# First stage of a decoder kernel: scores over 64 rows in pairs of banks, outputs in one bank, and a power on GpSimd for root and reciprocal

## The reference

```python
r, k, v, g = xr @ w_r.T, xk @ w_k.T, xv @ w_v.T, silu(xg @ w_g.T)   # xr.. are x mixed with x one token back
# per head, in chunks of tokens:
y = rr @ kk * Wmat @ vv + rr @ state * wb        # scores, masked by decay, times values; plus the carried state
state = ws * state + kk * wk @ vv
mu, var = y.mean(-1), y.var(-1)                  # over the 16 channels of a head
y = (y - mu) / jnp.sqrt(var + EPS)
y = y * ln_g + ln_b
y = y * g
x = _layernorm(x + y @ w_o.T)
```

## Time and profile before

| | us |
|---|---|
| three runs | 2878.19, 2883.38, 2891.40; median 2883.38 |
| the profiled execution, own time | 2882.24 |
| its span, from the first to the last instruction | 2880.9 |
| first stage, from the span's start | 0 to 279.5 |
| TensorE, VectorE, ScalarE, GpSimd busy in the first stage | 227.8, 183.9, 53.3, 69.3 |
| TensorE, VectorE, ScalarE, GpSimd busy in the whole span | 2227.3, 1720.4, 1181.4, 598.3 |

### The profile page before, as it was taken

The page is one execution under the profiler, slowest core; times in us unless marked ns, Lnnn a source line. Parts: engine busy times, 40 slices in busy tenths (PEclk is TensorE's granted clock), DMA queues, the critical chain, the costliest instruction groups (busy, mean ns, idle before and its releaser), DMA issues. The chain is left out here.

```text
span 2880.9 us, 41338 instructions
## 1 busy us (share of the span) xinstructions
PE 2227.3 (77%) x15516; PEld 1433.2 (50%) x15582; DVE 1720.4 (60%) x3425; ACT 1181.4 (41%) x2185; POOL 598.3 (21%) x488
## 2 busy tenths in 40 slices
PE   6995469897506999365589999996787787778777
PEld 3553137674404888334235555554455544455534
DVE  5676975467783333357456666661677652677663
ACT  2121664334331333121223555554566442566443
POOL 2220000001173455501310000000322142322052
PEclk9997579999657999687779999997899898899999
DMA  3001400100161111212431111102000001000000
GB/s 108 1 1 31 136 1 1 44 1 1 45 228 45 45 46 45 70 29 44 132 106 36 35 33 27 35 13 88 1 1 1 11 1 58 1 1 1 17 31 23
DMA packets 75010, 113.28 MB, mean 39 GB/s; under 512 B 22853, under 2 KB 59681, under 8 KB 74145
## 3 DMA queue, kind: packets, MB, share of 16 engines
q1 hardware_dynamic: 71744, 102.24, 11.8%
q0 software_dynamic: 3072, 8.39, 0.9%
HBM read 85.38 MB, written 31.20 MB: 40 GB/s over the span
## 5 line engine op out<-in xcount | busy, mean ns | idle before, releaser
L2338 DVE TENSOR_REDUCE xa_max<-psum 128x1 f32<-128x1024 f32 (+1 forms) x256 | 248.5, 988 | 130.0 <-PE psum L2211 129.3
L2444 ACT ACTIVATE xa_work<-psum 128x1024 f32<-128x1024 f32 (+1 forms) x208 | 212.7, 1023 | 188.6 <-PE psum L2234 186.7
L2249 PE MATMUL psum<-xa_work,xa_values 128*33 128x128 f32 (+1 forms) x3328 | 224.0, 277 | 0.0
L2249 PEld LDWEIGHTS psum<-xa_work,xa_values 128*33 128x33 f32 (+1 forms) x3328 | 168.1, 111 | 73.7 <-issue 70.2
L2644 PE MATMUL psum<-wqkv_l,x_hl_l 128*128 128x512 bf16 x538 | 136.9, 400 | 65.7 <-POOL x_hl_l L2904 32.9
L3010 PE MATMUL psum<-h_ch_f,w_f 128*128 128x512 bf16 (+1 forms) x556 | 134.9, 396 | 34.3 <-issue 13.1
L1623 DVE TENSOR_SCALAR moe_raw<-psum,tile_b 128x256 f32<-128x256 f32 x184 | 78.3, 475 | 138.9 <-PE psum L1465 137.9
L1719 POOL TENSOR_TENSOR x_ch<-moe_raw,x_ch 128x512 bf16<-128x512 f32 x92 | 105.4, 1156 | 151.9 <-ACT x_ch L1679 149.9
L1465 PE MATMUL psum<-moe_rows,moe_w 128*128 128x256 bf16 x1104 | 132.5, 278 | 3.0 <-POOL moe_rows L1715 3.0
L2234 PE MATMUL psum<-xa_query_rows,xa_key_rows 98*128 98x512 bf16 (+1 forms) x416 | 127.2, 388 | 8.4 <-ACT xa_work L2444 7.7
L2211 PE MATMUL psum<-xa_key_rows,xa_query_rows 96*128 96x512 bf16 (+1 forms) x512 | 127.0, 344 | 4.5 <-DVE xa_max L2338 2.4
(11 more groups left out here) (415 smaller groups left out, 4934.7 us busy)
## 6 DMA issues: line engine op xcount, KB each, us to landing
xa_key_rows<-cross_keys SPq DMA_DIRECT2D x48, 200.1 KB, 3.5
moe_raw<-in_moe_w SPq DMA_DIRECT2D x16, 512.0 KB, 4.8
x_ch<-in_moe_w SPq DMA_DIRECT2D x16, 512.0 KB, 4.7
cross_keys<-xa_work SPq DMA_DIRECT2D x4, 1601.0 KB, 5.7
moe_rows<-slots_in SPq DMA_DIRECT2D x23, 256.0 KB, 2.8
slots_out<-moe_rows SPq DMA_DIRECT2D x23, 256.0 KB, 2.1
ctx_f<-in_ctxT SPq DMA_DIRECT2D x2, 2401.5 KB, 15.3
xa_work<-in_ctxT SPq DMA_DIRECT2D x4, 800.5 KB
```

The lines of the kernel that those rows point to most:

```text
L2249: ins = pe.matmul(total.ap[a * LANE:a * LANE + VC, c:c + PIECE], t["v"][b][0:rows, kt, first + a, :], exps[0:rows, a, c:c + PIECE], start= ...
L2338: v.tensor_reduce(t["maxes"][n % 2][:, qt * HU + a, part:part + 1], u.wide[:, 0:c1 - c0], AX.X, ALU.max).then_inc(*u.free)
L2444: act.activation(t["exps"][k % EXPS][0:rows], u.wide[0:rows].rearrange("p (m q) -> p m q", q=T), ACT.Exp, scale=1.0 / float(np.sqrt(np.flo ...
```

## The change

Three edits, all in the first stage. The plan of `attend` goes by half of a time tile instead of by four heads; "score" is now two matmuls over 64 rows each, one on partitions 0 to 63 (the first four heads of the half) and one on 64 to 127 (the other four), into banks 0 and 1 or 2 and 3. For that GpSimd's `r_heads` holds four copies instead of eight, with the mask `head4`, in which copy a keeps head a and head a+4. Outputs go to bank 4 alone, and `a_masked` is a ring of four. The product's four matmuls go in the order 0, 2, 1, 3. In the finish, ScalarE only scales and adds (Identity), and GpSimd raises 128x512 to the power -0.5; the "invert" steps are gone.

```diff
     def attend(b):
+        products = lambda n: [("product", b, n // 2, 2 * (n % 2) + x) for x in range(2)]
         steps = []
...
+        for n in range(2 * TPB):
+            steps.append([("heads", b, k // 2, k % 2) for k in ((0, 1) if n == 0 else (n + 1,)) if k < 2 * TPB]
+                         + [("score", b, n // 2, n % 2)])
+            if n:
+                steps.append([("open", b, n // 2)] * (n % 2) + products(n - 1))
+        return steps + [products(2 * TPB - 1)]
...
-                + [[("invert", b, h, n)] for h in range(2) for n in range(2)] + [[("gated", b, h)] for h in range(2)]
+                + [[("gated", b, h)] for h in range(2)]
...
-        use.update(m.banks([p for p in plan if p[0] == "score"], (0, 1, 2)))
-        use.update(m.banks([p for p in plan if p[0] == "open"], (3, 4), signalled=False))
+        use.update(m.banks([p + (x,) for p in plan if p[0] == "score" for x in range(2)], (0, 1, 2, 3)))
+        use.update(m.banks([p for p in plan if p[0] == "open"], (4,), signalled=False))
...
-            pe.wait_ge(*u.empty)
-            pe.matmul(u.ap, t["k_ch"][b % 2][:, h, c * P:(c + 1) * P],
-                      t["r_heads"][(nth - 1) % 3][:, 4 * (q % 2):4 * (q % 2) + 4, :], start=True, stop=True).then_inc(*u.fill)
+            pe.wait_ge(*s.headed(nth))
+            for x in range(2):
+                pe.wait_ge(*use[step + (x,)].empty)
+            for x in range(2):
+                u, rows = use[step + (x,)], slice(x * P // 2, (x + 1) * P // 2)
+                pe.matmul(u.ap, t["k_ch"][b % 2][rows, h, c * P:(c + 1) * P], t["r_heads"][(nth - 1) % 3][rows, :, :],
+                          start=True, stop=True).then_inc(*u.fill)
...
-            for a in range(4):
+            for a in (0, 2, 1, 3):
...
-        elif kind == "invert":
-            b, h, n = step[1:]
-            part = t["std"][:, h, n * T // 2:(n + 1) * T // 2]
-            v.wait_ge(*use["variance", b, h].done)
-            v.reciprocal(part, part).then_inc(*s.inverted.up())
...
-            act.activation(t["std"][:, h, :], use[step].ap, ACT.Sqrt, scale=1.0 / N0, bias=m.eps[:, 2:3]).then_inc(*use[step].free)
+            act.activation(t["rstd"][:, h, :], use[step].ap, ACT.Identity, scale=1.0 / N0, bias=m.eps[:, 2:3]).then_inc(*use[step].free)
...
-            g.tensor_tensor(t["r_heads"][n % 3][:], t["r_ch"][b % 2][:, h, c * P:(c + 1) * P].unsqueeze(1).to_broadcast([P, 8, P]),
-                            m.const("head16").unsqueeze(2).to_broadcast([P, 8, P]), ALU.mult).then_inc(*s.headed.up())
+            g.tensor_tensor(t["r_heads"][n % 3][:], t["r_ch"][b % 2][:, h, c * P:(c + 1) * P].unsqueeze(1).to_broadcast([P, 4, P]),
+                            t["head4"][:].unsqueeze(2).to_broadcast([P, 4, P]), ALU.mult).then_inc(*s.headed.up())
+        elif kind == "variance":
+            b, h = step[1:]
+            part = t["rstd"][:, h, :]
+            g.wait_ge(*use[step].done)
+            g.tensor_tensor(part, part, t["power"][:].to_broadcast([P, T]), ALU.pow).then_inc(*s.inverted.up())
```

More of the change, by code:

```diff
@@ L298, in rwkv @@
                       "decays masks tables v_zero headed r_state zeroed state_read updated v_step multiplied "
-                      "squared inverted gated added variance deviation normed")
+                      "squared halved exponent inverted gated added variance deviation normed")
         general = [("receptance", 2), ("key", 2), ("key_tok", 2), ("value", 2), ("gate", 2), ("center", 1),
@@ L416, in rwkv_pe @@
             y_bank = use["open", b, c].ap
-            masked = t["a_masked"][(at["score", b, c, q] - 1) % 3]
-            pe.wait_ge(*use["score", b, c, q].done)
-            for a in range(4):
+            masked = t["a_masked"][(2 * (at["score", b, c, q // 2] - 1) + q % 2) % 4]
+            pe.wait_ge(*use["score", b, c, q // 2, q % 2].done)
+            for a in (0, 2, 1, 3):
                 p, x = divmod(4 * q + a, 2)
@@ L530, in rwkv_dve @@
         elif kind == "score":
[L531 to L537, removed]
+            b, c, h = step[1:]
+            for x in range(2):
+                u, n, q = use[step + (x,)], 2 * (at[step] - 1) + x, 2 * h + x
+                if n > 3:
+                    v.wait_ge(*s.multiplied(n - 3))
+                v.wait_ge(*u.full)
+                v.tensor_tensor(t["a_masked"][n % 4][:], u.ap.rearrange("p (a t) -> p a t", t=P),
+                                t["wmat"][:, 4 * q:4 * q + 4, :], ALU.mult).then_inc(*u.free)
         elif kind == "center":
@@ L598, in rwkv_act @@
                 elif kind == "key":
-                    act.wait_ge(*use["score", b - 2, TPB - 1, 3].full)
+                    for x in range(2):
+                        act.wait_ge(*use["score", b - 2, TPB - 1, 1, x].full)
                 else:
@@ L654, in rwkv_pool @@
         g.memset(t["v_tok"][n][:, :, :, 1, :], 0.0).then_inc(*s.v_zero.up())
+    g.memset(t["power"][:], -0.5).then_inc(*s.exponent.up())
+    g.wait_ge(*s.exponent.now())
     for step in plan:
@@ L658, in rwkv_pool @@
             g.wait_ge(*s.params(48))
+            g.tensor_tensor(t["head4"][:], m.const("head16")[:, 0:4], m.const("head16")[:, 4:8], ALU.add).then_inc(*s.halved.up())
+            g.wait_ge(*s.halved.now())
             g.wait_ge(*s.decays(1))
@@ L668, in rwkv_pool @@
                 ob, oc = divmod((n - 3) // 2, TPB)
-                g.wait_ge(*use["score", ob, oc, 2 * ((n - 3) % 2) + 1].full)
-            g.tensor_tensor(t["r_heads"][n % 3][:], t["r_ch"][b % 2][:, h, c * P:(c + 1) * P].unsqueeze(1).to_broadcast([P, 8, P]),
-                            m.const("head16").unsqueeze(2).to_broadcast([P, 8, P]), ALU.mult).then_inc(*s.headed.up())
+                for x in range(2):
+                    g.wait_ge(*use["score", ob, oc, (n - 3) % 2, x].full)
+            g.tensor_tensor(t["r_heads"][n % 3][:], t["r_ch"][b % 2][:, h, c * P:(c + 1) * P].unsqueeze(1).to_broadcast([P, 4, P]),
[5 more added lines that the diff above has]
+            g.tensor_tensor(part, part, t["power"][:].to_broadcast([P, T]), ALU.pow).then_inc(*s.inverted.up())
         elif kind == "open":
```

29 lines of the change are left out of this document (7 added, 22 removed).

## The result

| | before | after |
|---|---|---|
| median of four runs, us | 2886.5 (2878.19 to 2891.4) | 3474.85 (3470.23 to 3477.25) |
| span of the profiled execution | 2880.9 | 3475.9 |
| end of the first stage (VectorE's last copy of the transposed rows) | 279.42 | 870.08 |

The ratio is 1.203 (95% interval 1.200 to 1.206). The forecast was 2858 us, its range 2843 to 2900. The stage ends 590.7 us later and the span is 595.0 longer, so all but 4.3 us is in the stage that was edited. So the experiments are compared by the **stage end**; the medians stand beside it.

What follows compares the result with a forecast made beforehand. TensorE was taken to bound the first stage, VectorE close behind in batches 1 and 2. Terms -29.4 + 0.5 + 2.9 - 1.0 + 3.0 = -24.0 us on 2882.24 gave 2858 us, range 2843 to 2900.

Steps and rivals of the forecast that it cites:

- The power is the unknown: GpSimd's power on 128x512 in the finish: between 1.0 and 10.4 us, taken as 3.5 like the reciprocal.
- the power is slow: Rival: a GpSimd power of 8.3 us or more makes the kernel 14 us slower or worse, at most 2913; chance 0.20.
- What the power does to the queue: Heads queued behind GpSimd's powers come late: TensorE stalls +0.5 us for batches 1 and 2 together, +2.9 in batch 3.
- X: Length in us of one GpSimd power over 512 columns, taken as 3.5.
- 2X - 8.0: Change of the tail after the last attention loop, with two powers replacing four reciprocals: -1.0 us at the forecast length.
- 8X - 52.0: The whole change in time for larger X, zero at X = 6.5.
- scores: First-stage score matmuls: two 64-row halves run side by side, so 128 records take the time of 64, 27.3 us less.
- changes of shape: TensorE's switches between full-array and 32-column forms: 14 fewer at 0.15 us each, 2.1 us less.
- product groups: The new order of the four product matmuls was costed at nothing; 32-column pads still use two lanes at a time.
- The sum on TensorE: Scores and changes of shape together save 29.4 us of TensorE's time in the first stage.
- One bank, nothing: A single output bank costs nothing: ScalarE's copy ends 0.5 us behind the products, covered by a 1.05 us score pair.
- VectorE beside the power, +3: A GpSimd power holds VectorE's two-SBUF-input operations for its whole length, costing 3 us (1 a batch), between 0 and 9.

Runs made afterwards that it cites:

- e3_product_for_power: The changed kernel with GpSimd's power replaced by a multiplication on the same operands, root and reciprocal left out; 2858.16 us, ratio 0.991.
- experiment 1: The changed kernel with the power taken out: Sqrt and reciprocals restored (2859.18 us, ratio 0.991), or a plain product in its place (2858.16 us, ratio 0.991).
- e1_root_back: The changed kernel with ScalarE's Sqrt and VectorE's four reciprocals back in place of the power; 2859.18 us against 2884.9, ratio 0.991.
- experiment 4: The changed kernel with each power replaced by a 128x4096 product into a scratch tile and a 128x512 product in place; 2895.72 us against 2875.24, ratio 1.007.

## Why the prediction was wrong

**The step that failed** is "The power is the unknown", in its bound from above: three steps at the reciprocal's 6.8 ns a column, 10.4 us, of which 3.5 was taken. The power takes 82.06 us, 160 ns a column, 24 times as long as the reciprocal's and 79 times as long as a product on the same engine (1.04 us in `e3_product_for_power` where VectorE doesn't hold it). The nearest row was taken for a bound. It is a row of another operation on another engine, and nothing in the trace showed that GpSimd's power is built from such steps. Without a row in kind the range had no honest upper end, and the rival "the power is slow" was capped at 2913 by the same bound. In its kind, a power too slow for the queue, that rival is what happened.

**What the power does to the queue** was right. With X = 82.06 the stalls come out at 2 x 157.3 + 160.0 = 474.6 us, measured 470.9; the tail at 2X - 8.0 = 156.1, measured 165.4 - 9.4 = 156.0. The whole formula, 8X - 52.0, gives 604.5 us, the stage 590.7. Of the 13.8 us in between 8.0 lie in the power's part (630.7 by the formula, 622.7 by experiment 1). Stalls that came out shorter are 3.7 of them. The others are a balance against `e1_root_back`: under the power TensorE waits 11.2 us less for the gated outputs of batches 1 to 3 and 3.4 less for masks, but waits 2.8 for the single output bank and is busy 8.1 longer (176.62 against 168.49, at a mean granted clock of 0.61 against 0.93). The remaining 5.6 of the 13.8 are these steps:

| term | forecast | measured |
|---|---|---|
| scores | -27.3 | -21.1 (32 x 0.66), with 0.20 a pair for the changes of shape |
| changes of shape | -2.1 | in the rows above and below, not separable |
| product groups | 0 | -17.6 |
| TensorE waits longer elsewhere | 0 | +8.5 (25.5 to 34.0) |
| sum without the power | -29.4 | -32.0 |
| VectorE held by the power | +3 | no more than 0.4 (TensorE's waits for mixes: 3.3 in the changed kernel, 2.9 in `e1_root_back`) |

**The sum on TensorE, -29.4 against -32.0, was right by luck.** The scores were 6 us too good. The products, costed at nothing since "the 32-column pads still use two lanes at a time", brought 17.6, because the step looked at the order of the four and not at the fact that two groups now stand back to back and cover four lanes. So TensorE's busy time fell by 40.5 us, not 29.4. And 8.5 us were given back in waits, 6.5 of them for the gated outputs of VectorE's finish (14.1 to 20.6) and 2.2 for mixes, which the prediction looked for only under the power. It read 2.8 us of waits for masked scores, while the same view of before (60 to 240 us) has a larger one, for the gated outputs:

```profile
PE psum L449 <- DVE y_ch L555: 4.7, 3, 2.8
```

The last 1.8 us of the difference are not traced to a place. That `e1_root_back` and `e3_product_for_power` measured 2859.18 and 2858.16 us, as the forecast's 2858, is the same luck.

**One bank, nothing:** right with root and reciprocals back (no wait for the copy of the outputs among TensorE's). In the changed kernel such a wait is 2.8 us in three places, one of them 2.2, and the same in `e3_product_for_power`. There experiment 1 shows the cause, which is the same in the changed kernel at 682.88 us: not the copy's own 0.4 us, but what stands in front of it in ScalarE's queue. The prediction priced the copy alone.

**VectorE beside the power, +3:** wrong in its cause. The earlier trace rows show a GpSimd *product* holding the mixes, and experiment 4 shows it at four times the length. The power does so only at its start. In the changed kernel four operations of VectorE with two SBUF inputs begin 0.07 to 0.63 us into a power and take 1.41 to 1.53 us in place of 0.75; all that begin 1.6 us or more into one take their usual time. None begins more than some 10 us into a power, so of the rest of its 82 us the runs say nothing.

**Not tried:** a power on VectorE, and a power with a scalar exponent on GpSimd.

## What to carry to other kernels

A price for which no row of the same operation on the same engine exists has no upper bound in a row of something else; time it alone, in one instruction of the real size, before the rest of the change hangs on it. A slow step in the queue of a helper engine costs twice its length wherever two of them stand in front of what the bottleneck needs, so look at what is queued behind it, not at the idle share of the engine. When several edits come together, split the gain by busy time and by waits: two terms that were mis-sized in opposite directions can add up to the forecast.

## What the runs showed of the hardware

- GpSimd's power of two tensors, fp32: 160 ns a column, the same for 1, 8, 32, 64 and 128 rows, proportional to the columns (20.75 us for 128, 82.0 for 512).
- A GpSimd product that reads and writes SBUF holds VectorE's operations with two SBUF inputs for its whole length (8.17 us for two mixes beside 7.32 of product); a power of 82.28 us holds one only at its start (1.53 us in place of 0.75 for a mix that begins 0.37 us into it), and from 1.6 to some 10 us into it no longer (1.40 for two mixes). The Trainium skill's rule for two such operations (SBUF — State Buffer, "Summary: rules for kernel authors") that the second to issue blocks fully until the first is done holds for the product and, past its start, not for the power.
- 32-column matmuls pass as many side by side as the group has lanes: 16 records of 128 columns in 1.00 us on two lanes, in 0.59 on four. Their order in the group makes no difference that shows (0.59 in both).
- A pair of 64-row fp32 matmuls of 512 columns on the two halves of the rows runs side by side: 1.06 us between full-array matmuls, which is what one full-array matmul takes (0.86) and 0.10 each for entering and leaving the shape.
